# Audio tower on one core: a new round order, a folded position weight and four-head value products

## The reference

```python
power = |rfft(frames * window)|**2                     # 51 bins
h = (log(power @ mel.T + 1e-6) @ dct.T) @ w_proj + b_proj
x = layernorm(h)                                       # residual around all of attention
h1 = rmsnorm(x) * norm1_w
q, k, v = h1 @ wq, h1 @ wk, h1 @ wv                    # 8 heads of 64, 64, 24
qw = einsum(q, w_pos)                                  # 32 numbers per head
scores = (q k^T + qw basis^T + u k^T + v_param w_pos basis^T) / 8
x = softmax(scores) v @ wo + bo + x
x = gelu(rmsnorm(x) * norm2_w @ w1 + b1) @ w2 + b2 + x
h = h + x
n = layernorm(h)
h = h + mixture_of_16_experts(n, top 1000 tokens each) + shared_expert(n)
```

## Time and profile before

| | |
|---|---|
| time, median of 3 runs | 2253.63 us (2253.34 to 2255.13) |
| the profiled execution | 2256.45 us, span 2254.7 us |
| mean granted clock of TensorE | 0.982 |
| busy PE, DVE, ACT, POOL, whole span | 2069.0, 1365.8, 1103.7, 704.0 us |
| tower, first DFT to last transposes on PE | 29.99 to 1237.65 us |
| feed-forward, first matmul to end | 1256.98 us to the end |

### The profile page before, as it was taken

One profiled execution on the slowest core, in us unless ns is written; L12 is line 12 of the kernel. 1 busy time (PEld: TensorE's weight loads), 2 busy tenths in 40 slices (PEclk: granted clock), 3 DMA queues, 4 the chain that ended last, 5 costly groups with the idle time before them and its releaser, 6 DMA issues. The chain is left out here.

```text
span 2254.7 us, 46810 instructions
## 1 busy us (share of the span) xinstructions
PE 2069.0 (92%) x13522; PEld 1700.7 (75%) x13522; DVE 1365.8 (61%) x3632; ACT 1103.7 (49%) x2680; POOL 704.0 (31%) x587
## 2 busy tenths in 40 slices
PE   2999999999999999999996699989999999999997
PEld 1677777777777777777774577778888888888886
DVE  1577767677776767677673577744555554555531
ACT  2677777767777777777763222122222222222221
POOL 0122122121212212121221000236665566665563
PEclk9899999999999999999997899999999999999998
DMA  5555655555555655555561633325454444454442
GB/s 142 156 146 147 168 143 163 148 158 151 151 163 144 167 147 155 150 156 161 143 165 50 161 103 102 93 54 89 91 97 77 73 78 88 91 98 76 73 80 31
DMA packets 317544, 272.43 MB, mean 121 GB/s; under 512 B 80740, under 2 KB 304822, under 8 KB 317494
## 3 DMA queue, kind: packets, MB, share of 16 engines
q1 hardware_dynamic: 238374, 235.01, 39.0%
q0 software_dynamic: 70656, 30.65, 9.6%
q10 hardware_dynamic: 8464, 6.15, 0.9%
HBM read 150.73 MB, written 120.54 MB: 120 GB/s over the span
## 5 line engine op out<-in xcount | busy, mean ns | idle before, releaser
L1134 POOL DMA_INDIRECT out<-ff_y,ff_idxs x128 | 261.8, 2045 | 245.5 <-DVE ff_y L1417 187.9
L1194 ACT ACTIVATE ff_sg<-ffp_g 128x500 f32<-128x500 f32 x192 | 112.9, 588 | 400.3 <-PE ffp_g L1529 369.9
L1121 POOL DMA_INDIRECT ff_xg<-xs_d,ff_idxg x128 | 205.1, 1603 | 297.1 <-issue 283.6
L468 ACT ACTIVATE sb_prob<-sb_ssb,sb_mx 125x250 f32<-125x250 f32 x512 | 253.1, 501 | 58.6 <-DVE sb_mx L562 58.6
L1541 PE MATMUL ffp_d<-ff_wd,ff_wide 128*125 128x192 f32 x1536 | 261.2, 327 | 16.0 <-DVE ff_wide L1404 15.2
L1404 DVE TENSOR_TENSOR ff_wide<-ff_sg,ffp_u 128x500 f32<-128x500 f32 x192 | 129.4, 674 | 221.1 <-PE ffp_u L1529 219.5
L1541 PEld LDWEIGHTS ffp_d<-ff_wd,ff_wide 128*125 128x125 f32 x1536 | 247.8, 188 | 19.9 <-issue 18.2
L1529 PE MATMUL ffp_g<-ff_xsp,ff_wsp 128*128 128x500 f32 x960 | 251.8, 392 | 1.6 <-DVE ff_xsp L1276 1.6
L1529 PE MATMUL ffp_u<-ff_xsp,ff_wsp 128*128 128x500 f32 x960 | 249.6, 390 | 0.0
L548 DVE COPY sb_ptsb<-ps_ptps 125x500 f32<-125x500 f32 x256 | 172.9, 675 | 123.8 <-PE ps_ptps L716 120.6
L1529 PEld LDWEIGHTS ffp_g<-ff_xsp,ff_wsp 128*128 128x128 f32 x960 | 180.2, 189 | 39.3 <-issue 2.7
(11 more groups left out here) (181 smaller groups left out, 3664.4 us busy)
## 6 DMA issues: line engine op xcount, KB each, us to landing
bias_d<-sb_rsb SPq DMA_DIRECT2D x256, 219.6 KB
sb_bsk<-bias_d SPq DMA_DIRECT2D x256, 218.8 KB
hx_d<-sb_hx SPq DMA_DIRECT2D x32, 336.0 KB
sb_hxl<-hx_d SPq DMA_DIRECT2D x32, 336.0 KB
ff_wd<-WdT SPq DMA_DIRECT2D x16, 576.0 KB
xs_d<-sb_xs SPq DMA_DIRECT2D x32, 238.0 KB
bias_d<-sb_rsb SPq DMA_DIRECT2D x256, 25.5 KB
sb_bsk<-bias_d SPq DMA_DIRECT2D x256, 25.4 KB
```

What stands on the lines that cost most here:

```text
L468: a.activation(prob[:, s % 2, t], ssb[:, s % 2, t], ACT.Exp, bias=mx[:, s % 2, t:t + 1], scale=-1.0, accum_out=rs[:, t, s:s + 1]).then_inc ...
L1121: g.indirect_dma_start(xg[:, t], None, xs_d[:, :], bass.IndirectOffsetOnAxis(idxg[:, t:t + 1], 0), bounds_check=last).then_inc(gat, 16)
L1134: g.indirect_dma_start(out_d[:, :], bass.IndirectOffsetOnAxis(idxs[:, t:t + 1], 0), y[:, t], None, bounds_check=last, compute_op=ALU.add). ...
```

## The change

The change rewrites the round. Its parts:

1. `qw` no longer comes from `qu`. At the start PE multiplies `wq` with `w_pos` (16 matmuls), ACT and DVE split the product into high and low part, and it is kept as 256 further columns of the split weights. In slots 1 and 5 five matmuls from the split `hsp` make `qw` of two pairs at once; DVE makes it by four operations on 64 partitions each.
2. The mfcc stage goes: `dct` times `w_proj` is made once as `wmel`, and the projection reads `logmel`. The four row-inverse matmuls become transposes.
3. `quad_values` replaces `pair_values`: four heads, four column strips, in slots 4 and 0. `ptsb` gets four buffers.
4. The order on every engine is new. On PE `probs_T` of the head before stands first in the slot, in even slots ahead of `pair_scores`; the projections of a pair follow the position terms. On DVE, in even slots, the copy of `ptps` stands ahead of the score reductions, in odd slots behind them and behind what makes `qw`. The reload of the exponential's table stands behind the position terms of slots 4 and 6. The value copies go from ACT to DVE, `xb` on POOL to slot 4, the last transposes of `bd` to slot 3.
5. The third part of `w1` gets the bank `tps` and follows the first two at once; one gelu load serves all three.
6. The shared expert's weights and first tokens are loaded in the pass in which attention has ended, and split in the last pass; `feed_forward` begins with them there.

```diff
@@ uses of the two banks
-        T_USES, C_USES, D_USES, Q_USES = 5, 5, 3, 18
-        QK_USE = [0, 4, 10, 14]
-        QW_USE = [1, 5, 11, 15]
+        T_USES, C_USES, D_USES, Q_USES = 4, 5, 3, 16
+        QK_USE = [0, 4, 9, 13]
+        QW_USE = [1, 10]
+        QW_SLOT = {1: 0, 5: 1}
@@ ACT, body
+                    if tables_stale:
+                        a.preload_act_table_set(EXP_SET)
...
-                        a.activation(logmel[:], tps[0:MELS, 0:FRAMES], ACT.Ln, bias=tiny[:, 0:1]).then_inc(t_ev, 1)
-
-                        a.preload_act_table_set(EXP_SET)
@@ DVE, body
+                    if s == 0:
+                        pt_copy(bc, HEADS - 1)
+                    if s > 0 and s % 2 == 0:
+                        pt_copy(bb_, s - 1)
...
+                        for i in range(2):
+                            p = 2 * QW_SLOT[s] + i
+                            v.tensor_scalar(qw[halves[i], i], qps[use % 2][halves[i], 0:FRAMES], cq[halves[i], p:p + 1], None, ALU.add).then_inc(qw_hi, 1)
+                        for i in range(2):
+                            p = 2 * QW_SLOT[s] + i
+                            dve.wait_ge(qw_hi, done + i + 1)
+                            v.scalar_tensor_tensor(out=qw[halves[1 - i], i], in0=qps[use % 2][halves[i], 0:FRAMES], scalar=cq[halves[i], p:p + 1],
+                                                   in1=qw[halves[i], i].bitcast(F32), op0=ALU.add, op1=ALU.subtract).then_inc(q_ev[use % 2], 1)
...
+                    if s % 2 == 1:
+                        pt_copy(bb_, s - 1)
@@ PE, start
+            for p in range(PAIRS):
+                for k in range(2):
+                    for i in range(2):
+                        rows = slice(64 * i, 64 * i + 64)
+                        m(folded(i, k)[:, p], wqT[rows, p, k * 128:(k + 1) * 128], wpz[rows, p, 0, i], start=True, stop=True)
+            m(qps[1][0:MELS, 0:D], dct[:], wproj[:], start=True, stop=True)
@@ PE, row inverses and values
-                            ins = m(tps[:, k * FRAMES + t * TP:k * FRAMES + (t + 1) * TP], each, ident[0:TP, 0:TP], start=True, stop=True)
+                            ins = nc.tensor.transpose(tps[:, k * FRAMES + t * TP:k * FRAMES + (t + 1) * TP], each, ident[0:TP, 0:TP])
...
+                    pe.wait_ge(pt_ev, HEADS * b + QUAD * (k + 1))
                     for j in range(NT):
-                        for i in range(2):
-                            c = VC * ((h + i) % QUAD)
-                            ins = m(otps[c:c + VC, h // QUAD], vz[:, j, h + i], ptsb[:, i, j], start=j == 0, stop=j == NT - 1)
+                        for i in range(QUAD):
+                            ins = m(otps[VC * i:VC * i + VC, k], vz[:, j, QUAD * k + i], ptsb[:, i, j], start=j == 0, stop=j == NT - 1)
@@ PE, body
+                    if bq is not None and s in QW_SLOT:
+                        use = QW_USE[QW_SLOT[s]]
+                        q_freed(pe, bq, use)
+                        col = ALL_COLS + 128 * QW_SLOT[s]
+                        for k, (wk, xp, xk) in enumerate(PARTS):
+                            ins = m(qps[use % 2][:, 0:FRAMES], wsp[:, wk, col:col + 128], hsp[:, xp, xk], start=k == 0, stop=k == len(PARTS) - 1)
+                        ins.then_inc(q_mm, 1)
+                    if s == 0:
+                        probs_T(bc, HEADS - 1)
+                    if s > 0:
+                        probs_T(bb_, s - 1)
                     if bb_ is not None and s % 2 == 0:
                         pair_scores(bb_, s // 2)
...
+                    if bq is not None and s == 0:
+                        qk(bq, 0)
                     if s == 0:
-                        probs_T(bc, HEADS - 1)
-                    if s > 0:
-                        probs_T(bb_, s - 1)
+                        quad_values(bc, 1)
@@ SP, in the pass in which attention has ended; ACT and DVE, last pass
+                if bb_ is None and bc is not None:
+                    load_shared()
...
+                if bc is None and bd is not None:
+                    shared_high()
...
+                if bc is None and bd is not None:
+                    shared_low()
```

More of the change, by code:

```diff
@@ L49 @@
 ALL_COLS = 2 * HEADS * DK + D + DFF
+POS_COLS = HEADS * N_POS
 SROW = 2 * 128 + EXPERTS
@@ L418, in body @@
                         g.tensor_tensor(d_y[:], d_v[:], power[:, 0:NT], ALU.pow).then_inc(d_ch, 1)
[L419 to L423, removed]
+                    if bd is not None and s == 4:
                         pool.wait_ge(d_ev, D_USES * bd + 3)
@@ L453, in body @@
                         a.activation(kk[:, p], ps[:, 1], ACT.Copy).then_inc(q_ev[QK_USE[p] % 2], 1)
+                    if bc is not None and s == 1:
+                        act.wait_ge(inv_mm, bc + 1)
+                        wait(act, ot_ev, bc)
+                        a.activation(inv_b[:], tps[:, 0:NK * FRAMES].rearrange("p (k n) -> p k n", k=NK), ACT.Copy).then_inc(inv_ev, 1)
                     br, pair = biases(s, bq, bb_)
@@ L492, in body @@
                             a.activation(h2sp[:, 0, k], ps[:, k], ACT.Copy, scale=n2w[:, k:k + 1]).then_inc(c_hi, 1)
+                    if bt is not None and s == 4:
+                        act.wait_ge(t_mm, T_USES * bt + 3)
+                        wait(act, hx_st, 32 * bt)
+                        a.activation(hx[:, :, 0:D], bank2(tps, D, TP), ACT.Copy).then_inc(t_ev, 1)
                     if bc is not None and s == 5:
@@ new lines, in body @@
+                    if bc is not None and s == 4:
+                        if bd is not None:
+                            pe.wait_ge(d_ev, D_USES * bd + 3)
+                        pe.wait_ge(c_ch, C_CHAIN * bc + C_CHAIN)
+                        pe.wait_ge(c_ev, C_USES * bc + 1)
+                        transposes(bank2(cps, FRAMES, 128), h2n, c_mm)
+                    if bq is not None and s == 4:
+                        qk(bq, 2)
+                    if s == 4:
+                        quad_values(bb_, 0)
@@ new lines, in body @@
+                    if bc is not None and s == 5:
+                        pe.wait_ge(c_ev, C_USES * bc + 2)
+                        ps = bank2(cps, FRAMES, 128)
+                        for j in range(DFF // 128):
+                            col = COLS["w1"][0] + j * 128
+                            if j == 2 and bt is not None:
+                                pe.wait_ge(t_ev, T_USES * bt + 3)
+                            for k, (wk, xp, xk) in enumerate(PARTS):
+                                ins = m(ps[:, j] if j < 2 else tps[:, 0:FRAMES], wsp[:, wk, col:col + 128], h2sp[:, xp, xk], start=k == 0, stop=k == len(PARTS) - 1)
+                            if j > 0:
+                                ins.then_inc(c_mm, 1)
```

478 lines of the change are left out of this document (236 added, 242 removed).

## The result

The changed kernel takes 2285.24 us (median of four runs, 2282.82 to 2286.68), the kernel before, on the same chip, 2253.49. The ratio is 1.0145, with a 95% interval of 1.0124 to 1.0165: slower by 1.5%. Forecast were 2225 us, a range up to 2262 and "faster". The profiled execution has a span of 2283.9 us.

What follows compares the result with a forecast made beforehand. TensorE was taken to bound the tower, with the `ptps` copies next. Savings of 17.6 us in 28 rounds, 8.5 at the hand-over and 3.7 in the drain, less 1.2 at the start, made 28.6: forecast 2225 us, range 2175 to 2262.

Steps and rivals of the forecast that it cites:

- What bounds the kernel: Tower: TensorE is the bound; its own work falls by 3.4 us a round to about 31.1.
- The walk: Tower round: four stretches between scores of two heads, summed on TensorE or the chain holding it up: 35.34 us against 35.97.
- `qw` operations: Slots 1 and 5: four 64-row VectorE operations making `qw` take 1.75 us, bounds 1.54 and 2.0.
- R to QK: TensorE, from the start of two heads' position terms to a pair's projections directly behind, which need a bank from ACT: 1.23 us.
- QV: TensorE, slots 0 and 4: probabilities times values, four heads in four column strips; 1.15 us a group, bounds 0.97 to 1.94.
- a round is then 7.64 + 9.72 + 7.73 + 10.25: Tower: stretches of slots 6 and 7, 0 and 1, 2 and 3, 4 and 5 add to 35.34 us.
- That PT now stands before S costs little by itself: Even slots: a head's probability transposes before two heads' scores cost little; exponentials end 1.5 us or more before the copy.
- (1): Rival: copies hold nobody up, TensorE stays the bound; round 32.6 us, total 2149; between this and forecast, or this: chance 0.18.
- (2): Rival, slower: head 0's copy behind `qw`, value products two strips at a time; round 37.0, total 2271 us; chance 0.12.
- (3): Rival: order and work cancel in the rounds, 35.97 us again; only the hand-over between stages gains, total 2243; chance 0.08.
- Outside the rounds: Before, between and after the full rounds: 8.5 us saved at the hand-over, 3.7 in the drain, 1.2 lost at the start.
- hand-over and drain: Tower to feed-forward saves 8.5 us (bounds 5 to 11); the earlier third w1 group saves 3.7 in the last passes.

Runs made afterwards that it cites:

- experiment 7: Changed kernel, but in slots 1 and 5 VectorE copies the even head's transposed probabilities out before it makes `qw`, TensorE order as changed: 2147.19 us, ratio 0.9511.
- experiment 5: Changed kernel with scores and position terms first again in even slots on TensorE only, VectorE order as changed: 2091.39 us, ratio 0.9262.
- experiments 4 and 5: Changed kernel with scores first again in even slots, on TensorE and VectorE: 2097.46 us; the same on TensorE alone: 2091.39 us.
- experiment 8: Kernel with scores first on both engines (2097 us), plus a made stall of about 1.2 us behind the gate matmuls in slot 1: 2173.93 us, ratio 0.9640.
- experiments 2 and 10: Changed kernel with three needless matmuls in slot 1's wait only: 2239.86 us; kernel with scores first on both engines, stalled about 1.1 us in slot 5: 2107.41 us.

## Why the prediction was wrong

**What bounds the kernel**: right. PE's own work fell as summed: it is busy for 31.1 us of a full-clock round, forecast 31.1.

**The walk**: right to 0.4 us in its sum, at full clock, where errors of up to 0.6 in single stretches cancel in part. From S to S in the round that holds 1013 us, where the clock is 1.00: 7.19 (slots 2 and 3, forecast 7.73), 10.82 (4 and 5, forecast 10.25), 7.76 (6 and 7, forecast 7.64), 9.93 (0 and 1, forecast 9.72). Sum 35.70, forecast 35.34. Too low were: the `qw` operations, 2.03 (614.39 to 616.42), their upper bound, and not 1.75, twice; R to QK, 1.32 and 1.40 instead of 1.23 in slots 6 and 0; the two evacuations before the table load, 1.08 instead of 0.95; a PT with S behind it, 0.6 instead of 0.5. Too high were v, 1.15 instead of 1.44, and QV, which runs four strips abreast: 0.98 (629.41 to 630.39) against the 1.15 that I took from the weight loads, and the sixteen weight loads keep the load path busy for 0.58, as eight did, not for 1.14. The Trainium skill, TensorEngine Tiling (Array Packing), Theoretical Speedup, had said up to four times; the trace agrees, sixteen records (eight matmuls) in the time of eight before. The waits are where they were put: 0.6 and 0.7 before QK, 1.1, 1.4 and 0.6 before PT(1), PT(5) and PT(7), forecast 0.7 twice and 1.0, 1.1 and 0.7. One more, 0.3 before w1, was not forecast.

**The step that failed** is the sum "a round is then 7.64 + 9.72 + 7.73 + 10.25". It priced every PE group by a row at clock 1.00, in a round that had just been given three more us of waits. The earlier trace rows show the clock at 1.00 with 1.5 us of waits a round; that it would stay there with 4 to 5 was never argued. It didn't: the 1.0 us that PE "waits" in slots 0 and 1 (1.10 measured) is the wait behind which the clock falls, in 24 rounds of 28. The measured round is 35.7 at full clock and 37.37 on the mean. So 1.67 us, the clock, and 0.36, the net of the terms above, are missing in each of 28 rounds: 57 us. That the clock follows what PE does was at hand: the prediction itself speaks of "the low clock" at the start, behind 24.80 us of idleness (the DFT group takes 1.16 us there, 0.65 at 607.89 in a full round), and uses it nowhere else. The Trainium skill has this as well, in TensorE: Matmul & The Clock Gate, A second HAM failure mode: psum-queue depth-cycling, where frequent short idle stretches between groups of matmuls send the clock back and forth between its two levels. The trace agrees in that the clock goes back and forth, 0.94 in the loop; the section gives no length for such a stretch, and here one of 1.1 us a round was enough.

**"That PT now stands before S costs little by itself"** was wrong too, in another way. The walk held its cost (the waits for the copies), but I put those down to the `qw` operations and to R before QK. That was half of it: with the `qw` operations behind the copy a round takes 32.9 (experiment 7). But experiment 5 shows that S and R ahead of PT would have hidden nearly all of the waits with the `qw` operations where they are: 35.7 at full clock, 31.0 with scores first. Of these 4.7 us the waits account for 1.1 + 1.4 + 0.6 before PT, 0.5 before QK (0.6 and 0.7 against 0.3 and 0.5) and 0.3 before w1. The other 0.8 is in PE's busy time, 31.07 in the one round and 30.16 in the other for the same matmuls: a group that is followed by a wait shows its last columns, which the next group otherwise overlaps.

**The rivals.** (1), PE as the bound with 32.6 us a round and 2149 in all, was said to be out of reach because R directly before QK costs 0.69 twice. With PT between them it costs 0.28 once; in slot 0 QK then waits 0.5 to 0.7 for DVE's low half of `hsp`. That version is what experiments 4 and 5 run, and it beats the rival's number. (2), slower, had the right sign and the wrong cause: QV doesn't run two strips at a time, and its point of decision, 36.5, is passed by the clock. (3) did not come. A rival on the clock was missing.

**Outside the rounds**: net 11.0 forecast, 10.4 measured, of parts that were off both ways; that the net agrees is luck. From the end of the 28 rounds on 20.9 were gained instead of the 12.2 of hand-over and drain together, 16.1 of them between the last row inverses and the first product (50.8 before, 34.7 after); the start and the first interval cost 10.5 instead of 1.2. The first DFT comes 3.2 later (33.15), not 7.0; it is the filling rounds that lose 7.3 where they were to gain 5.8. The clock is lower there too: 0.84 from 60 us to the second row-inverse group, 0.92 before. What lowers it there was not tried.

## What to carry to other kernels

An idle stretch of TensorE can cost more than its length, here two and a half times (2.8 us for 1.14, where the clock fell). Before summing a walk that trades work for waits, look at where the waits fall and what stands before them, and price the groups behind each of about a microsecond or more at the lower clock, as a case of its own (here it was not the longest one that cost). Between two hand-overs of one buffer put the work that doesn't need it: an order that runs the dependent step first can turn a change worth 7% into one that loses 1.5%. The best version here is the change with scores first on TensorE, 2091 us.

## What the runs showed of the hardware

A wait of TensorE of 1.1 us behind transposes and sixteen-column matmuls brought its clock down to 1.2 GHz for about 3.5 to 7 us, in 24 of 28 rounds of the changed kernel and of experiment 8; one of 1.0 to 1.4 us behind 250-column matmuls did not (experiments 2 and 10). Which of the two, the work before the wait or its place in the round, decides is not shown. Three needless matmuls in the first wait, 1.1 us of work, made the kernel 45 us faster. I had expected neither that waits of about one microsecond matter nor that it depends on the place.
